# Merging the first two rounds of a staged attention and expert kernel, with two weight products made once

## The chip, the cores and the metric

The kernel runs on one core of a Trainium2 chip (trn2). The metric is the device time of one execution in microseconds, as the median of several runs. The engines are TensorE (PE, with its weight loads shown as PEld), VectorE (DVE), ScalarE (ACT), GpSimd (POOL) and SyncE (SP), which here only issues DMAs. Each runs its own list of instructions in order; they wait for one another through semaphores.

## The reference

The input x is 8 batches of 512 tokens of width 128. Two blocks follow one another, each with a normalisation ahead and one behind, and a residual sum:

```
x = x + layernorm(attn(layernorm(x)))        # block A: one head of 128, rotary, causal
x = x + layernorm(ffn(layernorm(x)))         # block B
attn: q, k = rope(x wq), rope(x wk);  r = softmax(mask(q k^T / 128)) (x wv) wo
ffn:  h = rmsnorm(x, g1);  c = h w_down (128 -> 64)
      q, k, v = c wq, c wk, c wv   (16 heads of 4 channels, rotary on q and k)
      x = x + softmax(mask(q k^T / 2)) v w_up
      t = rmsnorm(x, g2);  the two best of 8 experts by softmax(t router_w), weights normalised
      y = x + sum over the two of gate * (silu(t w1) * (t w3)) w2      (128 -> 256 -> 128)
```

All products are in float32 except the 16-head scores, which use bfloat16 rows in which each float32 value is cut into three parts.

## The kernel before

The work on a batch is cut into four stages, named by a letter: **a** is block A's attention up to the normalised result; **p** is block B's normalisation, the 64-wide projections, rotary, the cut into bfloat16 parts, the turned queries and keys, and the row maxima of the first group of four heads; **m** is the 16-head attention's scores (maxima m_x, exponentials m_e, in four groups g of six jobs each, m_xgn and m_egs) and the first half of the value products; **f** is the rest of those products, w_up, the router, and the sending of token rows to DRAM sorted by expert. A tile phase then runs the experts over tiles of 128 rows and finishes the batches.

The stages are software pipelined over rounds. Round i does stage a of batch i, p of batch i-1, m of batch i-2 and f of batch i-3, as far as they exist. The rounds are "a", "ap", "apm", "apmf" (five times, four of them in a loop of two by two), "pmf" (m of batch 6), "mf" (m of batch 7, called the drain round below) and "f" (with tiles between). Eleven rounds in all.

In each round every engine works through a hand-written list of steps (ORDER for full rounds; FILL_ORDER, SECOND_ORDER, LEAD_ORDER, TRAIL_ORDER, DRAIN_ORDER, LAST_ORDER for "a", "ap", "apm", "pmf", "mf", "f"). A step named in several lists is one job: TensorE makes it into a PSUM bank, and ScalarE or VectorE empties it. There are two small banks (for all steps but scores), given out in turn in TensorE's order, and three wide ones for scores. A matmul step waits until its bank was emptied by the job two before it (small) or three before it (wide). "warmN" is N matmuls of ones that nobody reads. "x&y" means that two score jobs are issued interleaved.

The steps that the change and the prediction name:

- a_xT turns the normalised x; a_qkv0 to 3 make q, k, v (TensorE L957, emptied by ScalarE L1145); a_rope is on VectorE for batches 0 and 1 (L706 to L712), else on POOL; a_qT, a_kT turn them; a_s0 to 3 are the scores (L971), their maxima on VectorE (L1508) and exponentials on ScalarE (L1162); a_p0 to 2 turn the probabilities (L979); a_oT multiplies them with v (L986), ScalarE empties it into a_xT, and a_r multiplies that with wo (L993); VectorE divides by the sums (L1520), and a_rstat and p_rnorm normalise (with a power on POOL, L1302, between).
- p_x1 (POOL L1321), p_stats, p_norm, p_hT (turned, L921, scaled by g1 on emptying), p_cT (times w_down, L1004, 64 rows of result), p_qkv0 and 1 (L1010), p_keep, p_rope and p_cut (L675 to L695; for batch 0 the keys' half on POOL and the queries' half on VectorE, for the others both on POOL), p_slots (POOL L1335: six copies of key parts into k_rows), p_slot0 to 2 (ScalarE L1199: query parts into q_rows), p_k0, p_k1, p_q0, p_q1 (turned rows, L1024), p_x0 to 5 (maxima, L1421).
- m_cutg writes the maxima of group g into q_rows (VectorE L1564), m_shiftg turns those rows (L1036, copied by VectorE L1569), and the exponentials of group g (ScalarE L1216) follow it. f_up's sum is L1581, the router's logits arrive at L1589.
- plan0 to plan2 in the drain round (VectorE L1703 to L1725) compute the table of the first 25 tiles. SyncE (L749 to L762) waits for the last exponential score of the pmf round, loads w1 and w3 (L750, L751) and w2 (L753, eight transfers), then waits for plan1 (soon_placed), writes the table to DRAM (L758), waits, and reads it back into one partition (L762). TensorE's plan_soon waits for that and for the weights, and then reads 25 expert numbers into registers:

```
sp.wait_ge(soon_placed, 1)
... tile_table <- soon_u; wait soon_out; early_u <- tile_table ...
def read_soon():                      # TensorE's step plan_soon
    pe.wait_ge(soon_in, 16 * 2)
    pe.wait_ge(weights_in, 16 * N_WEIGHTS)
    experts.update(read_tiles(pe, 1, 0, EARLY, NE - 1))
```

## Time and profile before

| | us |
|---|---|
| Median of 3 runs | 697.23 (695.5 to 699.96) |
| The profiled execution, its own time | 696.38 |
| Its span in the profile | 694.2 |
| PE busy | 609.9 (88%) |
| DVE busy | 506.8 (73%) |
| ACT busy | 412.0 (59%) |
| POOL busy | 339.6 (49%) |

The span runs from the first to the last instruction; 2.2 us of the execution lie around it. Busy time of PE is modelled from pipelined matmuls, so a busy PE is not PE at its peak, and it counts the warm-up matmuls. "PEclk" is the granted clock of TensorE as a share of full speed (1.00 is 2.4 GHz, 0.50 is 1.2 GHz). A row of the timeline gives start, duration, engine, line, operation, what it writes and reads, its shape and how often it stands in a row; in brackets is the idle time of the engine before it, and what ended it. A float32 product shows as two instructions.

### The profile page before, as it was taken

The page shows a single profiled execution, that of the slowest core. Times are in us where ns is not written, and L with a number is a line of the kernel's source. Part 1 is how long each engine was busy: PE and PEld are TensorE (multiplying, and loading weights), DVE is VectorE, ACT ScalarE, POOL GpSimd, SP SyncE. Part 2 cuts the span into 40 slices and gives each one's busy share as a digit, 9 for nine tenths or more (in the row PEclk, how much of TensorE's full clock was granted, in tenths as well). Part 3 has the DMA queues.
Part 4 walks back from the last instruction along what each step waited for, and adds up shares of the span by engine and source line. Part 5 has one row for each costly group of instructions (what it writes and reads, how often), then busy time and mean ns, then how long its engine had stood idle before and what let it go on. Part 6 is the DMA issues. An engine that isn't in the chain of part 4 may idle for free.

```text
span 694.2 us, 15645 instructions
## 1 busy us (share of the span) xinstructions
PE 609.9 (88%) x5186; PEld 364.6 (53%) x5186; DVE 506.8 (73%) x1616; ACT 412.0 (59%) x826; POOL 339.6 (49%) x388
## 2 busy tenths in 40 slices
PE   8887599999999899999999999879998887899980
PEld 3444345455545455454544545434343486899970
DVE  4456877786897898689779878677688356457894
ACT  3223158566658656565765657454564676688971
POOL 0043246058527835752873565165014056767783
PEclk9988879999999999999999999977898999999995
DMA  6200000000100000010000001001232013345653
GB/s 174 78 0 1 0 1 1 2 1 1 35 2 1 14 23 1 1 35 3 1 19 19 1 1 35 2 2 36 77 109 70 14 58 111 99 113 166 176 156 91
DMA packets 35616, 30.05 MB, mean 43 GB/s; under 512 B 6160, under 2 KB 32720, under 8 KB 35520
## 3 DMA queue, kind: packets, MB, share of 16 engines
q1 hardware_dynamic: 31216, 19.65, 10.1%
q0 software_dynamic: 4320, 9.38, 4.0%
q8 instruction: 45, 0.74, 0.4%
q14 instruction: 35, 0.29, 0.1%
HBM read 17.54 MB, written 12.57 MB: 43 GB/s over the span
## 4 chain that ended last, share of the span: by engine, by line
PE 64%; DVE 14%; ACT 9%; issue 7%; POOL 5%; DVEq 0%; POOLq 0%; ACTq 0%
PE wide L1116 9%; PE small L933 7%; PE small L921 5%; PE wide L895 4%; PE wide L1125 4%; ACT pT L1216 4%; PE wide L868 4%; PE wide L886 4%; PE wide L843 3%; PE small L957 3%; PE wide L877 3%; PE small L986 3%; PE small L971 2%; DVE nmax L1421 2%; PE small L1010 2%
## 5 line engine op out<-in xcount | busy, mean ns | idle before, releaser
L1421 DVE TENSOR_REDUCE nmax<-wide 128x2 f32<-128x256 f32 (+3 forms) x256 | 200.1, 817 | 43.7 <-PE wide L886 42.5
L1216 ACT ACTIVATE pT<-wide 128x1024 f32<-128x1024 f32 (+1 forms) x192 | 161.6, 883 | 41.3 <-PE wide L895 40.4
L1360 POOL DMA_INDIRECT result_rows<-k_rows,dest x71 | 69.9, 984 | 49.5 <-DVE k_rows L1764 26.6
L933 PE MATMUL small<-pT,v_pad 128*5 128x512 f32 (+3 forms) x1024 | 85.2, 478 | 2.7 <-ACT pT L1216 2.7
L1351 POOL DMA_INDIRECT token_rows<-m_row,place_u x64 | 62.5, 977 | 45.4 <-issue 16.4
L1302 POOL TENSOR_TENSOR a_rstd<-a_ve,neg_half 128x4 f32<-128x4 f32 x16 | 16.5, 1029 | 117.3 <-DVE a_ve L1407 117.3
L895 PE MATMUL wide<-qT,kT 32*128 32x384 bf16 (+3 forms) x512 | 71.5, 312 | 0.0
L886 PE MATMUL wide<-kT,qT 32*128 32x256 bf16 (+3 forms) x512 | 70.5, 314 | 0.0
L877 PE MATMUL wide<-future_T,idb 128*128 128x128 bf16 (+1 forms) x384 | 62.6, 246 | 7.9 <-DVE nmax L1421 4.6
L868 PE MATMUL wide<-future_sb,idb 128*128 128x128 bf16 (+1 forms) x384 | 64.1, 250 | 5.7 <-ACT pT L1216 2.8
L1145 ACT ACTIVATE oT_g<-small 128x512 f32<-128x512 f32 x32 | 19.1, 597 | 79.7 <-PE small L933 79.7
L933 PEld LDWEIGHTS small<-pT,v_pad 128*5 128x5 f32 x1024 | 25.8, 92 | 59.8 <-issue 50.3
L1759 DVE TENSOR_TENSOR a_work<-a_work,wide 128x256 f32<-128x256 f32 x71 | 29.7, 418 | 32.6 <-PE wide L1125 16.7
L877 PEld LDWEIGHTS wide<-future_T,idb 128*128 128x128 bf16 x384 | 28.6, 99 | 36.4 <-issue 15.8
L1125 PE MATMUL wide<-a_p_sb,a_work 128*128 x284 | 43.2, 275 | 0.6 <-DVE k_rows L1764 0.6
L1116 PE MATMUL wide<-a_work,p_hT_sb 128*128 128x128 f32 x280 | 38.0, 279 | 4.8 <-ACT a_work L1242 3.5
L868 PEld LDWEIGHTS wide<-future_sb,idb 128*128 128x128 bf16 x384 | 29.8, 101 | 22.7 <-issue 11.5
L1116 PE MATMUL wide<-a_work 128*128 128x128 f32 x288 | 38.8, 278 | 2.4 <-issue 2.2
L1125 PEld LDWEIGHTS wide<-a_p_sb,a_work 128*128 128x128 f32 x284 | 37.3, 192 | 0.8 <-issue 0.8
L1116 PEld LDWEIGHTS wide<-a_work,p_hT_sb 128*128 128x128 f32 x280 | 34.0, 192 | 7.0 <-ACT a_work L1242 4.4
L1116 PEld LDWEIGHTS wide<-a_work 128*128 128x128 f32 x288 | 35.3, 193 | 3.4 <-issue 3.0
L895 PEld LDWEIGHTS wide<-qT,kT 32*128 32x128 bf16 x512 | 20.1, 92 | 29.6 <-issue 16.8
(254 smaller groups left out, 1260.6 us busy)
## 6 DMA issues: line engine op xcount, KB each, us to landing
a_qkv_sb<-token_rows SPq DMA_DIRECT2D x71, 72.0 KB, 1.8
x<-L_attn_x SPq DMA_DIRECT2D x8, 256.0 KB, 3.4
w<-L_ffn_w SPq DMA_DIRECT2D x2, 1024.0 KB, 7.3
out<-x SPq DMA_DIRECT2D x16, 128.0 KB
result_rows<-k_rows,dest POOLq DMA_INDIRECT x71, 2.6
token_rows<-m_row,place_u POOLq DMA_INDIRECT x64
a_p_sb<-L_ffn_w SPq DMA_DIRECT2D x8, 128.0 KB, 4.6
yin_own<-result_rows SPq DMA_DIRECT2D x8, 128.0 KB
```

The lines of the kernel that those rows point to most:

```text
L868: pe.matmul(bank[:, i * T + lo:i * T + lo + len(blocks) * P], idb[:, :], future_sb[:, 0:len(blocks), :], start=True, stop=False, skip_grou ...
L877: pe.matmul(diagonal, idb[:, :], future_T[:, :, :] if len(blocks) > 1 else future_T[:, 0, :], start=True, stop=False, skip_group_check=True)
L886: return pe.matmul(bank_of(ring, max_name(g, n))[:, at:at + keys], qT1[rows, m.parity, g, tile * P:(tile + 1) * P], kT[rows, m.parity, g, ...
L895: return pe.matmul(bank_of(ring, exp_name(g, s))[:, at:at + queries_from(tile)], kT[rows, m.parity, g, tile * P:(tile + 1) * P], qT2[rows, ...
L921: last = pe.transpose(bank[0:rows, t * P:(t + 1) * P], source(t), ident)
L933: last = pe.matmul(bank[32 * r:32 * r + HD + 1, k * P:T], v_pad[:, m.parity, k, g * R + r, :], probs, start=(k == 0), stop=(k == NT - 1), ...
L1116: last = pe.matmul(wide[:, tile.half, j * P:(j + 1) * P], w_now[tile.half][:, j * P:(j + 1) * P], x_T[:, tile.half, :], start=True, stop=True)
L1125: last = pe.matmul(y_bank(tile), hid_T[:, tile.half, h * P:(h + 1) * P], w2_sb[:, e, h, :], start=(h == 0), stop=(h == FH - 1))
L1216: act.activation(pT[:, g % 2, part, at:at + n].rearrange("p (n q) -> p n q", n=2), in_, ACT.Exp, scale=SCALE_B).then_inc(ring.free(step), 1)
L1351: pool.indirect_dma_start(token_rows[:, :], bass.IndirectOffsetOnAxis(ap=place_u[:, n, t:t + 1], axis=0), m_row[:, n, t, :], None).then_in ...
L1360: pool.indirect_dma_start(result_rows[:, :], bass.IndirectOffsetOnAxis(ap=dest[:, tile.buf:tile.buf + 1], axis=0), y_rows[:, tile.buf, :], ...
L1421: ins = dve.tensor_reduce(nmax[:, tile, heads], bank[:, :, at:at + keys_up_to(tile)], AX, ALU.max, negate=True)
```

## The change

Four things are changed together.

1. The rounds "a" and "ap" are one round, "bap": b is stage a of batch 0, a is stage a of batch 1, and p is stage p of batch 0. The "a" list's steps of batch 0 are named b_... and mapped by of_first. Ten rounds remain. In this round VectorE has the keys' half of p_rope and p_cut and also the six key copies (p_slots), POOL has the queries' half.
2. fold0 makes wv wo once (turn wv, copy, multiply, copy; TensorE and ScalarE take turns), so that v already holds v wo. a_oT is gone, and a_r is ten products of 128x128x128 with the probabilities as the stationary operand. fold1 makes w_down [wq wk wv] once into wqkv_f (128x192). p_cT is gone, and p_qkv multiplies p_hT with wqkv_f.
3. wo is loaded with the first group of weights, ahead of the cosine and sine tables; batch 1's x has a semaphore of its own (x_second).
4. The lists of all rounds but "f" are laid anew. In the drain round plan_soon moves from the end of TensorE's list to the place behind m_e01, and plan1 on VectorE from behind m_shift1 to behind m_cut0.

The diff, cut to its core (the POOL and ACT lists of the other rounds, and the ends of long ones, are left out):

```diff
 ORDER = {   "PE"
-        m_x1_0 m_shift0 f_pv2 f_o1 m_e00&m_x1_1 f_pv3 f_o2 m_e01&m_x1_2 m_x1_3 a_xT f_o3 m_x1_4 a_qkv0 m_x1_5
-        f_oT a_qkv1 a_qkv2 a_qkv3 m_e02&m_x2_0 f_up p_hT m_x2_1 m_shift1 m_e03 m_e04 p_cT m_e05&m_x2_2 p_qkv0
-        a_qT m_x2_3 f_tT m_e10&m_x2_4 m_e11 f_logits p_qkv1 a_kT m_e12&m_x2_5 m_pv0 a_s0 m_e13 a_s1 m_e14 m_e15
-        a_s2 a_s3 f_rank m_x3_0 m_x3_1 m_pv1 m_shift2 m_x3_2 a_p0 m_e20 m_e21 p_k0 m_e22&m_x3_3 p_k1 p_q0
+        m_x1_0 m_shift0 f_pv2 f_o1 m_e00&m_x1_1 f_pv3 m_e01&m_x1_2 f_o2 m_x1_3 a_xT f_o3 m_x1_4 a_qkv0 a_qkv1
+        a_qkv2 a_qkv3 m_e02&m_x1_5 f_oT m_e03 f_up m_x2_0 m_x2_1 m_shift1 p_hT m_x2_2 p_qkv0 m_e04&m_x2_3 m_e05
+        f_tT m_e10&m_x2_4 f_logits m_e11 p_qkv1 m_e12&m_x2_5 a_qT a_kT m_pv0 m_e13 a_s0 a_s1 a_s2 a_s3 m_e14
+        m_e15&m_x3_0 m_x3_1 f_rank m_pv1 m_shift2 a_p0 m_e20&m_x3_2 m_e21 p_k0 m_e22&m_x3_3 p_k1 p_q0
...
-FILL_ORDER = {   "PE"
-        warm18 warm11 a_xT a_qkv0 a_qkv1 a_qkv2 a_qkv3 warm5 a_qT warm3 warm2 a_kT a_s0 a_s1 warm1 a_s2 a_s3
-        warm7 a_p0 a_p1 warm1 a_p2 warm2 a_oT warm3 a_r warm35
-SECOND_ORDER = {   "PE"
-        warm1 warm2 warm4 warm4 p_hT p_cT p_qkv0 p_qkv1 a_xT a_qkv0 a_qkv1 a_qkv2 warm5 a_qkv3 p_k0 warm3 p_k1
-        warm2 p_q0 warm1 a_qT p_q1 a_kT warm3 a_s0 a_s1 p_x0 warm1 a_s2 a_s3 p_x1 p_x2 warm2 p_x3 a_p0 a_p1
-        warm1 a_p2 p_x4 a_oT p_x5 a_r
...
+FIRST_ORDER = {
+    "PE": """
+        warm18 fold0 b_xT b_qkv0 b_qkv1 b_qkv2 b_qkv3 warm11 warm5 b_qT b_kT warm3 b_s0 b_s1 warm2 b_s2 b_s3
+        a_xT b_p0 b_p1 warm1 b_p2 b_r warm3 warm2 warm1 warm2 a_qkv0 a_qkv1 warm5 warm5 fold1 warm5 a_qkv2
+        a_qkv3 p_hT warm1 p_qkv0 p_qkv1 warm5 warm2 a_qT a_kT a_s0 a_s1 warm5 a_s2 a_s3 warm5 warm3 a_p0 warm2
+        warm1 warm3 a_p1 p_k0 a_p2 p_k1 p_q0 p_q1 a_r p_x0 p_x1 warm1 p_x2 p_x3 p_x4 p_x5""",
+    "ACT": """
+        fold0 b_xT b_qkv0 b_qkv1 b_qkv2 b_qkv3 b_qT b_s0 b_s1 b_s2 b_s3 a_xT b_p0 b_p2 fold1 a_qkv0 a_qkv1
+        a_qkv2 a_qkv3 p_hT p_keep p_qkv0 p_qkv1 a_qT a_s0 a_s1 p_slot0 p_slot1 a_s2 a_s3 p_slot2 a_p0 a_p2 p_q0
+        p_q1""",
+    "DVE": """
+        b_stats b_norm a_stats a_norm b_rope b_kT b_s0 b_s1 b_s2 b_s3 b_p1 b_r b_rstat p_rnorm p_stats p_norm
+        p_ms a_rope a_kT a_s0 a_s1 p_rope a_s2 a_s3 p_cut p_slots a_p1 p_k0 p_k1 a_r p_x0 a_rstat p_x1 p_x2 p_x3
+        p_x4 p_x5""",
+    "POOL": """
+        b_rstd a_rstd b_rrstd p_x1 p_rstd p_rs p_rope p_cut p_slots a_rrstd""",
 LEAD_ORDER = {   "PE", then "DVE"
-        m_x1_0 m_x1_1 a_xT m_x1_2 a_qkv0 m_x1_3 m_x1_4 m_shift0 a_qkv1 m_x1_5 a_qkv2 a_qkv3 m_e00&m_x2_0 m_x2_1
+        m_x1_0 m_shift0 m_x1_1 m_x1_2 a_xT m_e00&m_x1_3 a_qkv0 p_hT m_e01 m_e02&m_x1_4 a_qkv1 a_qkv2 m_x1_5
...
-        m_cut0 m_x1_0 p_rnorm a_stats p_stats a_norm m_x1_1 m_x1_2 p_norm m_x1_3 p_ms m_shift0 a_rope m_x1_4
+        p_rnorm m_cut0 a_stats m_x1_0 m_shift0 p_stats a_norm m_x1_1 p_norm m_x1_2 m_x1_3 m_x1_4 p_ms m_x1_5
 TRAIL_ORDER = {   "PE", then "DVE"
-        m_x1_0 m_shift0 f_pv2 f_o1 m_e00&m_x1_1 f_pv3 f_o2 f_o3 m_e01&m_x1_2 f_oT m_x1_3 p_hT f_up m_x1_4 p_cT
-        m_e02&m_x1_5 p_qkv0 p_qkv1 m_x2_0 f_tT m_shift1 f_logits m_e03&m_x2_1 m_e04 m_e05 m_e10 m_e11
+        m_x1_0 f_pv2 m_shift0 f_o1 m_e00&m_x1_1 f_pv3 m_e01&m_x1_2 f_o2 m_e02 f_o3 m_x1_3 f_oT m_e03&m_x1_4 f_up
+        m_e04&m_x1_5 m_e05 p_hT p_qkv0 p_qkv1 f_tT f_logits m_x2_0 m_x2_1 m_pv0 f_rank m_x2_2 m_x2_3 m_x2_4
+        m_shift1 m_e10&m_x2_5 m_e11 p_k0 m_x3_0 m_e12&m_x3_1 p_k1 m_e13&m_x3_2 m_e14 m_shift2 m_x3_3
...
+        p_rnorm m_cut0 m_shift0 p_stats m_x1_0 f_o1 m_x1_1 p_norm f_o2 f_o3 m_x1_2 m_x1_3 m_x1_4 p_ms f_up
+        m_x1_5 f_ms m_cut1 f_logits f_route0 p_rope f_route1 m_x2_0 f_route2 f_route3 f_at f_rank m_x2_1 m_x2_2
 DRAIN_ORDER = {   "PE", then "DVE"
-        f_pv2 f_o1 m_x1_0 m_x1_1 f_pv3 m_shift0 m_x1_2 f_o2 f_o3 m_e00&m_x1_3 m_x1_4 f_oT m_e01&m_x1_5 f_up
-        m_x2_0 m_e02&m_x2_1 m_e03 m_shift1 m_x2_2 m_e04&m_x2_3 f_tT m_e05 m_e10 m_e11 m_e12 m_e13 f_logits m_e14
...
-        m_e22 m_e23 m_shift3 m_e24 m_e25 m_e30 m_e31 m_e32 m_e33 m_o0 m_e34 m_e35 plan_soon""",
+        f_pv2 m_x1_0 f_o1 m_shift0 m_x1_1 f_pv3 f_o2 m_e00&m_x1_2 m_e01 plan_soon f_o3 m_e02&m_x1_3 m_x1_4 f_oT
+        m_e03&m_x1_5 f_up m_e04 m_e05 m_shift1 m_x2_0 m_pv0 m_e10 f_tT m_e11 m_e12 f_logits m_e13 m_e14
+        m_e15&m_x2_1 m_x2_2 m_x2_3 f_rank m_pv1 m_x2_4 m_x2_5 m_x3_0 m_shift2 m_x3_1 m_o0 m_e20&m_x3_2 m_x3_3
...
-        plan0 m_cut0 m_x1_0 f_o1 m_x1_1 m_shift0 m_x1_2 f_o2 f_o3 m_x1_3 m_x1_4 m_x1_5 f_up m_cut1 m_x2_0 f_ms
-        m_x2_1 m_x2_2 m_x2_3 m_shift1 plan1 f_logits f_route0 f_route1 f_route2 f_route3 f_at m_x2_4 f_rank
+        plan0 m_cut0 plan1 f_o1 m_x1_0 m_x1_1 m_shift0 f_o2 m_x1_2 f_o3 m_x1_3 m_x1_4 m_x1_5 f_up m_cut1
+        m_shift1 f_ms m_x2_0 f_logits f_route0 f_route1 f_route2 f_route3 f_at f_rank f_count m_x2_1 m_x2_2
+def of_first(step, a, ring):
+    return ("a" + step[1:], Batch(0, 0), ring.of_first()) if step[0] == "b" else (step, a, ring)
-        FIRST = ("a", "ap", "apm", "apmf")
+        FIRST = ("bap", "apm", "apmf")
+        FOLDS = ((wqkv_a[:, 2 * D:3 * D], m_tT[:, 0:P], wo_sb[:, :], wqkv_a[:, 2 * D:3 * D], P, D),
+                 (wdown_sb[:, :], oT_sb[:, 0:P], wqkv_b[:, :], wqkv_f[:, :], L, 3 * L))
+        def key_slots(eng, p):
+            k = k_rows[:, :, :, :, :].rearrange("p t h s d -> p (t h) s d")
+            for b, slots in ((part1, (0, 3, 5)), (part2, (1, 4)), (part3, (2,))):
+                for s in slots:
+                    last = eng.tensor_copy(k[:, :, s, :], b[:, 1, :, :])
+            last.then_inc(S["p_rows"], 1)
+            def fold(n):                                        (TensorE)
+                left_, turned, right, _, rows, cols = FOLDS[n]
+                pe.wait_ge(*((first_in, 16 * N_FIRST), (consts_in, 16 * N_CONSTS))[n])
+                pe.transpose(wide[0:rows, 1 + n, 0:P], left_, idf[:, :]).then_inc(folded, 1)
+                pe.wait_ge(folded, 4 * n + 2)
+                pe.matmul(wide[:, 1 + n, T:T + cols], turned, right, start=True, stop=True).then_inc(folded, 1)
-                    elif step == "a_oT":
...
+                    elif step == "a_r":
                         bank = take(ring, step, ["a_p0", "a_p1", "a_p2"])
+                        for i in range(NT):
+                            for k in range(i + 1):
+                                n, at = ((0, 0), (1, 0), (2, 0), (1, 3 * P))[k]
+                                at += (i - k) * P
+                                last = pe.matmul(bank[:, i * P:(i + 1) * P], a_pT[:, n, at:at + P],
+                                                 a_qkv[:, k, 2 * D:3 * D], start=(k == 0), stop=(k == i),
+                                                 skip_group_check=True)
-                    elif step == "p_cT":
-                        bank = take(ring, step, ["p_hT"])
-                        full(ring, step, pe.matmul(bank[0:L, :], wdown_sb[:, :], p_hT[:, :], start=True, stop=True))
-                            last = pe.matmul(bank[:, at:at + 3 * L], p_cT[:, t * P:(t + 1) * P], wqkv_b[:, :],
+                            last = pe.matmul(bank[:, at:at + 3 * L], p_hT[:, t * P:(t + 1) * P], wqkv_f[:, :],
+            def fold(n):                                        (ScalarE)
+                _, turned, _, product, rows, cols = FOLDS[n]
+                act.wait_ge(folded, 4 * n + 1)
+                act.activation(turned, wide[0:rows, 1 + n, 0:P], ACT.Copy).then_inc(folded, 1)
+                act.wait_ge(folded, 4 * n + 3)
+                act.activation(product, wide[:, 1 + n, T:T + cols], ACT.Copy).then_inc(folded, 1)
```

## Rows read from the trace of the kernel before

**Rows 1.** Busy time by stretch: span, busy us (instructions), PEclk, DMA, GB/s.
```profile
0.00:36.00 36.00, 30.34 (x129) 14.80 (x130) 15.81 (x55) 10.40 (x19) 2.32 (x7) 1.00 0.41 121
36.00:80.83 44.83, 36.28 (x188) 20.18 (x186) 29.67 (x82) 14.67 (x33) 13.32 (x20) 0.89 0.00 1
80.83:136.66 55.83, 48.32 (x408) 24.97 (x408) 41.58 (x103) 34.21 (x59) 23.96 (x30) 0.88 0.01 1
...
197.02:255.85 58.83, 55.24 (x518) 30.12 (x518) 49.48 (x138) 38.27 (x73) 34.55 (x40) 1.00 0.04 11
...
436.57:497.50 60.93, 52.78 (x459) 24.22 (x458) 42.49 (x101) 31.69 (x56) 25.78 (x31) 0.80 0.04 11
497.50:543.60 46.10, 41.03 (x388) 17.66 (x386) 35.55 (x116) 24.67 (x40) 10.87 (x11) 0.89 0.31 96
...
```

**Rows 2.** TensorE timeline; last, instructions of L1145 (ns min/median/max, starts).
```profile
246.74 2.42 PE L986 MATMUL small<-a_work,a_qkv_sb 128*128 128x512 f32 x8
...
252.39 1.16 PE L993 MATMUL small<-wo_sb,a_xT_sb 128*128 128x128 f32 x8
...
215.28 1.07 PE L1004 MATMUL small<-p_hT_sb,wdown_sb 128*64 128x512 f32 x2
...
L1145 ACT ACTIVATE p_cT_sb<-small x8: 573/591/592, 45.2 to 453.5; 64x512 f32<-64x512 f32 x8
```

**Rows 3.** Timeline of the first two rounds.
```profile
14.67 0.69 DVE L706 TENSOR_TENSOR a_work<-a_qkv_sb,cos_a_sb 128x512 f32<-128x512 f32 x1 [5.63 <-ACT a_qkv_sb L1145]
...
32.48 0.69 DVE L1520 TENSOR_TENSOR a_xn<-small,a_ri 128x512 f32<-128x512 f32 x1 [4.79 <-PE small L993]
...
45.98 2.10 PE L1010 MATMUL small<-wqkv_b_sb,p_cT_sb 64*128 64x192 f32 x8 [0.77 <-ACT p_cT_sb L1145]
...
55.83 3.42 POOL L1335 COPY k_rows<-part 128x256 bf16<-128x256 bf16 x6
```

**Rows 4.** Timeline of VectorE: two casts of 128x256, without and beside POOL's work.
```profile
8.75 0.28 DVE L1434 CAST future_T<-pT 128x256 bf16<-128x256 f32 x1
...
53.27 0.57 DVE L691 CAST part<-p_t 128x256 bf16<-128x256 f32 x1
```

**Rows 5.** Busy time by stretch within the third round.
```profile
80.83:86.00 5.17, 0.00 (x0) 0.00 (x0) 4.93 (x25) 0.00 (x0) 3.30 (x3) 0.51 0.00 0
86.00:98.00 12.00, 10.56 (x50) 5.10 (x51) 9.04 (x24) 3.98 (x7) 2.86 (x3) 0.64 0.01 2
```

**Rows 6.** Timeline of ScalarE: the first exponential of all.
```profile
97.10 1.02 ACT L1216 ACTIVATE pT<-wide 128x1024 f32<-128x1024 f32 x1
```

**Rows 7.** Busy time by stretch within the pmf round.
```profile
459.00:478.00 19.00, 16.79 (x117) 6.90 (x118) 13.57 (x36) 7.98 (x11) 15.28 (x21) 0.55 0.04 13
```

**Rows 8.** Timeline of VectorE in the drain round: f_up's sum, and the logits.
```profile
510.94 0.69 DVE L1581 TENSOR_TENSOR res<-small,res 128x512 f32<-128x512 f32 x1
...
520.31 0.19 DVE L1589 COPY lgs<-small 128x32 f32<-128x32 f32 x1 [0.44 <-PE small L1059]
```

**Rows 9.** Timeline of SyncE in the drain round; then its waits (us, times, longest).
```profile
498.81 8.05 SPq L753 DMA_DIRECT2D a_p_sb<-L_ffn_w  x8
...
525.39 0.51 SPq L762 DMA_DIRECT2D a_qkv_sb<-tile_table  x2
...
SPq L762 <- DMA tile_table<-a_xT_sb: 4.8, 1, 4.8
...
SPq L639 <- DMA a_qkv_sb<-tile_table: 2.1, 1, 2.1
```

**Rows 10.** Timeline of VectorE in the drain round: m_cut0, and plan1's first and last.
```profile
500.85 0.23 DVE L1564 TENSOR_TENSOR q_rows<-nmax 128x16 bf16<-128x16 f32 x1
...
516.62 0.18 DVE L1667 TENSOR_TENSOR a_kT_sb<-a_kT_sb 128x32 f32<-128x32 f32 x1
...
519.72 0.14 DVE L1696 TENSOR_SCALAR a_xT_sb<-a_xT_sb 128x1 uint32<-128x1 f32 x1
```

**Rows 11.** Timeline of TensorE in the tile phase, where it reads 24 registers.
```profile
589.64 1.13 PE L1116 MATMUL wide<-a_work 128*128 128x128 f32 x8 [1.87 <-issue]
```

200 lines of the change are left out of this document (100 added, 100 removed).

## The prediction

> **What bounds the kernel now.** I first cut the span into rounds at the first cut of the maxima (m_cut0, L1564) of each batch and read the busy time by stage [rows 1]. The stages have different limits. In a full round (all four stages; there are five, and the one shown is typical of 58.8 to 60.8 us) TensorE is busy 55.24 of 58.83 us at a granted clock of 1.00, with VectorE at 49.48 and ScalarE at 38.27: there a microsecond less of TensorE work is nearly a microsecond of time. The first two rounds are another thing: 36.00 us and 44.83 us in which VectorE works 15.81 and 29.67 us; one batch's chain of dependent steps sets them, and 117 warm-up matmuls fill much of TensorE's row. The third round (80.83 to 136.66) and the pmf round (436.57 to 497.50) show a clock of 0.88 and 0.80, so they lose time to gaps and to the clock after them. In the drain round (mf) VectorE is busy 35.55 of 46.10 us, and the last exponentials follow its maxima. The tile phase, all that lies behind 543.6, is not touched: its list is the same and its inputs come in the same form.
>
> **Less TensorE work in each round.** a_oT and a_r (eight and eight instructions, 2.42 and 1.16 us [rows 2]) become one a_r of ten 128x128x128 products, or twenty instructions. The row of 1.16 us has eight of this shape, 0.145 each: 20 x 0.145 = 2.9 us against 3.58, so -0.7. The step p_cT (1.07 us) goes whole; p_qkv keeps its eight instructions of 192 columns, only with 128 rows contracted in place of 64. No row shows that form; the nearest with 128 rows is the one of 0.145 for 128 columns, so 0.22 for 192 and 1.7 for eight, against the 2.10 that the eight take at 45.98 at a lower clock [rows 3]: no loss is in sight, and I take no change. That is -1.8 us in a round with a and p. ScalarE loses the evacuations of a_oT and p_cT (0.59 us each [rows 2]) and their two hand-overs; it isn't the bound, so I count these at nothing in a full round. VectorE keeps its work, which was 49.5 of 58.8 us, so it does not become the bound at 57 us. Five full rounds: 5 x -1.8 = -9. From below and above: -3.5 if new gaps (the four a_s jobs now stand back to back on TensorE with two small banks between them) eat 1.1 us a round, and -12 if the hand-overs count too.
>
> **The merged first round.** The old chain of batch 0: a_r reaches VectorE at 32.48, p_qkv runs at 45.98, the keys' slots are copied on POOL from 55.83 for 3.42 us, and the stage ends with m_cut0 at 80.83 [rows 1, 3]. In the new list fold0 (a transposition, a copy, a product, a copy, some 1.5 us) stands after 18 warm-ups in place of 29, so batch 0's transposes start about 0.6 us earlier, if wo, now the fifth transfer of the first group, has landed; its issue moves ahead of the two tables. Dropping a_oT takes its evacuation and hand-overs, 1.1 us, besides the 0.7. With a_xT of batch 1 ahead of b_p0 on ScalarE costing back 0.6, a_r arrives at about 30.8 (-1.6). Without p_cT (1.07 + 0.59 + two hand-overs of 0.2) p_qkv moves by 3.5 in all. But then VectorE has batch 1's work in the way: a_rope (14.67 to 18.75 for batch 0, so 4.1 us), a_kT, a_s0 and a_s1 stand ahead of p_rope, and p_cut and the six key copies follow it on VectorE. Adding these up from 41.3: rope to 45.4, a_kT to 48.2, a_s1 to 50.4, p_rope to 52.9, a_s2 and a_s3 to 54.4, p_cut to 57.5. The six copies on VectorE aren't in the trace: a cast of 128x256 there took 0.28 us with POOL idle and 0.57 beside POOL's work [rows 4], so 1.7 to 3.4 us; POOL has finished its half by then, so I take 2 and have them at 59.5, where the old kernel had 59.25. After that p_k, p_q, a_r and a_rstat and the six p_x maxima (6.3 us) follow in a row, with nothing of the next round between: p_x5 at about 75.5. So the merge brings -5.3, not the 10 that the overlap of two 36 to 45 us rounds suggests, because VectorE's list is serial. Bounds: -3 (copies at 0.57, p_x waiting on a_r's 2.9 us of matmuls) to -9 (VectorE waits less than I put).
>
> **Third round.** In the first 5.17 us TensorE did nothing, then it ran 12.00 us at a clock of 0.64 [rows 5]: its list held m_shift0 back behind a_qkv0, so the first exponential came at 97.10, 16.3 us into the round [rows 6]. Now m_shift0 is second, p_rnorm is done early, and m_e00 stands right after a_xT, which needs VectorE's a_stats, p_stats and a_norm, some 7 us. Filling the gap and the clock's loss (12.00 x 0.36 = 4.3) is worth up to 9.5 with the 1.8 of work; a_xT still waits, so I take half, -5 (0 to -9).
>
> **The pmf round.** It has no a stage and yet lasts 60.93 us, longer than a full round. From 459 to 478 the clock was 0.55 [rows 7]: 16.79 us busy, some 7 more than at full clock. p_cT's 1.07 goes; m_e02 to m_e05 come earlier, so that TensorE has denser work up to the p stage, but f_logits on VectorE now follows m_cut1 with only m_x1_5 and f_ms before it, and must wait for the row-norm chain (9.4 us from f_up's sum to the logits in the drain round [rows 8]). Gains and this wait partly cancel: -5 (+2 to -11).
>
> **The drain round, the part that goes the wrong way.** plan_soon was TensorE's last step; now it stands after m_e01. It waits for the tile table to have been through DRAM. The table can't be early: SyncE issues the eight w2 transfers until 506.86, and only then looks at the table. From its two writes, some 0.65 us of issue, it waited 4.8 us for them, took 0.51 to issue the second trip and 2.1 until it landed [rows 9]: 506.9 + 8.1 = 515.0, or 17.5 us after the round's start at 497.5. TensorE gets there sooner: plan0 ends with m_cut0 at 500.85, plan1 takes 516.62 to 519.86, so 3.2 us [rows 10], moved ahead of f_o1: VectorE is through with it at 504.3. One o-normalisation (0.5), two maxima of about 1.2 and a copy of 0.4 make 507.8, and TensorE's f_o2, m_e00 with m_x1_2, and m_e01 (estimates from the same timeline: the small ones 0.6 each, the pair 1.4) make 510.4. So TensorE stands still for 4.6 us and then reads 25 registers; the gap in the tile phase where 24 are read was 1.87 us [rows 11]. Queued behind it on TensorE are f_o3, m_e02, m_x1_3 and all maxima, and so VectorE and ScalarE, which run dry after m_x1_2 and m_e01. That is +6.5. Before, this reading lay beside the last exponentials and cost nothing. Also the wait for the logits loses its cover, since m_x2_1 to m_x2_5 now follow f_count: I add 2 (up to 5), less 0.5 for the register reads that leave the end. Drain: +8 (+3 to +12).
>
> The Trainium skill ("DMA: Bandwidth & Descriptors", Anatomy of one DMA) says that a DMA has about 2.0 us of fixed cost, most of it the receipt of the write. By that page the two trips would take about 4 us behind their issues and not 6.9, and the drain would cost about 5 in place of 8. For the trip back this trace agrees (2.1 us); for the one into DRAM it doesn't (4.8 us), and the measurement decides.
>
> **The sum** goes against the profiled execution, 696.38 us with a span of 694.2: -5.3 - 5 - 9 - 5 + 8 = -16.3, a span of 677.9, and 2.2 around it give 680.1. The median of the runs, 697.23, is 0.85 above the profiled one, so 681.
>
> **Rivals.** *The drain's wait is hidden* (0.17): TensorE arrives at plan_soon later than I put, or what it delays isn't needed. For it: TensorE idled 5 of 46 us there before. Then 681 - 8 = 673. *Only the removed work counts* (0.20): the new lists bring nothing in the third and pmf rounds beyond 1.8 and 1.1 us. Against it stands the clock of 0.51 and 0.64; for it, that a chain through VectorE (41.6 of 55.8 us busy) binds anyway. -5.3 - 1.8 - 9 - 1.1 + 8 = -9.2, or 688. *Slower, by the clock in the full rounds* (0.07): there TensorE idled 3.6 us of 58.8 in short pieces at a clock of 1.00. The relaid lists put p_hT directly before p_qkv0 and a_s0 to a_s3 together, and with less work the pieces grow; after longer gaps (80.83 to 86) the trace shows a stretch at 0.64, and after those around 457 one at 0.55. 55.24 us of work at a mean clock of 0.88 as in the third round costs 7.5 us more, five times 37; it needs 16.3 + 7 = 23.3, or 4.7 us in each of five rounds (a clock near 0.92), to come out slower by 1%. Then 704 and more. The Trainium skill ("TensorE: Matmul & The Clock Gate", Part 1) has the clock throttled by default and released by activity, which is what this rival would need and what the two slow stretches agree with.
>
> **Chances and range.** Forecast 0.56, hidden wait 0.17, only the work 0.20, slower 0.07. The forecast's own bounds (full rounds -3.5 to -12, merge -3 to -9, third 0 to -9, pmf +2 to -11, drain +3 to +12) added as independent errors give about 10 either way, 671 to 691. With the other cases I say 668 to 694. Faster by over 1% (about what a measurement of this kernel can tell from no change), under 690.3: 0.80; within 1%: 0.13; slower: 0.07.
>
> **What would show it.** Right: full rounds of about 57.5 us; no instruction of p_cT or a_oT and twenty of 0.145 in a_r; m_cut0 of batch 0 near 75.5; its first exponential within 10 us of that; TensorE idle for 4 to 7 us some 13 us into the drain round, ended by the DMA of the tile table. Wrong: full rounds still at 59 or more (the list made new gaps), a drain round of 46 us, or a granted clock under 0.95 in the full rounds.

## The result, and the profile after

The changed kernel is slower: 712.16 us (median of 4 runs, 707.98 to 714.79) against 697.27 for the kernel before (4 runs beside it); ratio 1.0205, 95% interval 1.0142 to 1.0267. The forecast was 681. Its profiled execution took 710.8 us with a span of 708.9, 14.7 more than the 694.2 of before.

First the busy time by stretch of the changed kernel, cut as in [rows 1]: at the m_cut0 of each batch, then the drain round and the tile phase. The columns are stretch and length, then busy us (instructions) of PE, PEld, DVE, ACT and POOL, then clock, DMA share and GB/s.

```profile
0.00:36.00 36.00, 30.41 (x137) 15.78 (x138) 19.96 (x75) 11.55 (x24) 4.59 (x9) 1.00 0.42 121
36.00:69.68 33.68, 24.82 (x162) 14.54 (x160) 24.91 (x72) 12.48 (x30) 8.49 (x12) 0.92 0.00 1
69.68:128.92 59.24, 51.28 (x414) 28.19 (x414) 39.72 (x99) 33.55 (x57) 22.89 (x29) 0.85 0.01 1
...
189.20:249.40 60.20, 54.81 (x520) 29.74 (x520) 51.99 (x137) 37.21 (x70) 33.83 (x40) 0.97 0.04 11
249.40:311.13 61.73, 55.41 (x520) 30.72 (x520) 51.83 (x138) 37.87 (x71) 34.98 (x41) 0.94 0.03 11
311.13:369.81 58.68, 53.12 (x520) 29.32 (x520) 51.79 (x138) 37.21 (x70) 34.38 (x40) 1.00 0.04 11
...
430.96:497.40 66.44, 51.81 (x454) 24.57 (x454) 39.44 (x97) 31.51 (x54) 24.77 (x30) 0.78 0.03 10
497.40:558.20 60.80, 48.78 (x390) 20.72 (x386) 37.30 (x122) 24.25 (x39) 10.86 (x11) 0.75 0.25 73
```

- The first m_cut0 is at 69.68 where it was at 80.83: -11.2 (forecast -5.3).
- Third round: 59.24 for 55.83, +3.4 (forecast -5).
- The five full rounds together: 302.0 for 299.9, +2.1 (forecast -9). TensorE's busy time did fall, 55.2 to 56.8 us a round before and 52.8 to 55.4 now; but its idle time rose from 3.7 to 6.6 us a round, and VectorE's busy time from about 49.2 to 51.8.
- pmf round: 66.44 for 60.93, +5.5 (forecast -5). Drain round: 60.80 for 46.10, +14.7 (forecast +8).
- Tile phase: 150.70 for 150.60.

The experiments are read from m_cut0 to m_cut0: by that cut pmf is +5.3 and all from the drain's m_cut0 to the end +15.0 (208.4 for 193.4), and the five terms make 14.7. One thing shifts this cut: in the new list of the pmf round p_rnorm stands ahead of m_cut0 on VectorE. The last full round takes 61.15 us with that list behind it (61.14 to 61.16 in e1, e2 and e8) and 58.98 with the old one (e5; 58.97 in e12), so some 2.2 us of the "five full" belong to the pmf round where its new list is run.

Next, the drain round of the changed kernel around plan_soon: SyncE's issues and TensorE.

```profile
504.53 3.94 PE L954 MATMUL small<-pT,v_pad 128*5 128x512 f32 x32 [2.82 <-DVE o_tok L1621]
505.97 0.72 SPq L779 DMA_DIRECT2D tile_table<-a_xT_sb  x2
509.91 0.39 PE L916 MATMUL wide<-qT,kT 32*128 32x512 bf16 x2
512.03 0.51 SPq L783 DMA_DIRECT2D a_qkv_sb<-tile_table  x2
516.62 1.57 SPq L793 DMA_DIRECT2D a_qkv_sb<-token_rows  x3
516.67 1.09 PE L942 MATMUL small<-idf,oT_g 128*128 128x128 f32 x4 [6.37 <-issue]
```

TensorE reached plan_soon at 510.3, stood still for 6.37 us and resumed at 516.67: the forecast had 510.4, and 4.6 plus 1.87 us. From the table's two writes SyncE waited 5.3 us before the trip back (4.8 in [rows 9]), then 1.9. The new item is the first line: plan1 stands ahead of f_o1 on VectorE, so f_pv3 waited 2.82 us for the o-normalisation and then ran at a granted clock of 0.59 (504.5 to 508.5), 3.94 us for 32 instructions that take 2.34 at full clock.

VectorE in the merged round:

```profile
29.34 0.69 DVE L1565 TENSOR_TENSOR a_xn<-small,a_ri 128x512 f32<-128x512 f32 x1 [2.90 <-PE small L1022]
...
39.56 0.69 DVE L727 TENSOR_TENSOR a_work<-a_qkv_sb,cos_a_sb 128x512 f32<-128x512 f32 x1
...
53.16 0.91 DVE L715 COPY k_rows<-part 128x256 bf16<-128x256 bf16 x6
...
61.23 1.21 DVE L1455 TENSOR_REDUCE nmax<-wide 128x2 f32<-128x1024 f32 x1
```

The first a_r arrived at 29.34 (put at 30.8), batch 1's a_rope began at 39.56 (41.3), the six key copies on VectorE took 0.91 us in all (2) and ended at 54.1 (59.5). From there to m_cut0 it was 15.6 us (16.0). The last line is the first maximum of stage p (p_x0), which begins that tail.

### The profile page after: what moved, and what is told of

Read it like the earlier page. It is cut to its first block, busy times and chain, and to the rows that moved or that the text cites. A ratio compares the mean times of both kernels' runs of the same rounds, so it can differ in the third digit from the quotient of the medians.

```text
span 708.9 us, 15634 instructions
## 1 busy us (share of the span) xinstructions
PE 596.0 (84%) x5182; PEld 362.4 (51%) x5182; DVE 515.1 (73%) x1622; ACT 406.2 (57%) x814; POOL 336.1 (47%) x381
## 4 chain that ended last, share of the span: by engine, by line
PE 47%; DVE 25%; issue 11%; ACT 6%; POOL 6%; SPq 2%; DMA 2%; DVEq 0%; POOLq 0%; ACTq 0%
DVE nmax L1455 7%; PE wide L1145 7%; PE small L954 5%; PE wide L916 4%; PE small L942 4%; PE wide L898 4%; PE wide L1154 3%; PE small L1022 3%; PE wide L889 3%; PE small L992 3%; ACT pT L1252 2%; PE small L1006 2%; PE wide L907 2%; PE small L1053 2%; DVE a_xn L1445 2%
## 5 line engine op out<-in xcount | busy, mean ns | idle before, releaser
L1252 ACT ACTIVATE pT<-wide 128x1024 f32<-128x1024 f32 (+1 forms) x192 | 163.5, 882 | 85.7 <-PE wide L916 84.2
L1394 POOL DMA_INDIRECT result_rows<-k_rows,dest x71 | 69.9, 984 | 54.2 <-DVE k_rows L1809 30.8
L907 PE MATMUL wide<-kT,qT 32*128 32x256 bf16 (+3 forms) x512 | 72.4, 321 | 0.0
L898 PE MATMUL wide<-future_T,idb 128*128 128x128 bf16 (+1 forms) x384 | 64.7, 253 | 8.0 <-DVE qT L1614 4.1
L1174 ACT ACTIVATE oT_g<-small 128x512 f32<-128x512 f32 x32 | 19.1, 597 | 64.9 <-PE small L954 64.8
L1804 DVE TENSOR_TENSOR a_work<-a_work,wide 128x256 f32<-128x256 f32 x71 | 29.7, 418 | 35.2 <-ACT a_work L1284 19.1
L1145 PE MATMUL wide<-a_work,p_hT_sb 128*128 128x128 f32 x280 | 38.0, 279 | 3.7 <-ACT a_work L1278 1.8
L1145 PE MATMUL wide<-a_work 128*128 128x128 f32 x288 | 38.7, 277 | 2.3 <-issue 2.1
L1145 PEld LDWEIGHTS wide<-a_work,p_hT_sb 128*128 128x128 f32 x280 | 34.0, 192 | 6.0 <-issue 3.7
L1145 PEld LDWEIGHTS wide<-a_work 128*128 128x128 f32 x288 | 35.1, 192 | 3.3 <-issue 2.9
```

The source lines that it names most:

```text
L898: pe.matmul(diagonal, idb[:, :], future_T[:, :, :] if len(blocks) > 1 else future_T[:, 0, :], start=True, stop=False, skip_group_check=True)
L907: return pe.matmul(bank_of(ring, max_name(g, n))[:, at:at + keys], qT1[rows, m.parity, g, tile * P:(tile + 1) * P], kT[rows, m.parity, g, ...
L1145: last = pe.matmul(wide[:, tile.half, j * P:(j + 1) * P], w_now[tile.half][:, j * P:(j + 1) * P], x_T[:, tile.half, :], start=True, stop=True)
L1252: act.activation(pT[:, g % 2, part, at:at + n].rearrange("p (n q) -> p n q", n=2), in_, ACT.Exp, scale=SCALE_B).then_inc(ring.free(step), 1)
L1394: pool.indirect_dma_start(result_rows[:, :], bass.IndirectOffsetOnAxis(ap=dest[:, tile.buf:tile.buf + 1], axis=0), y_rows[:, tile.buf, :], ...
L1804: dve.tensor_tensor(hid_T[:, tile.half, :], silu[:, tile.half, :], wide[:, tile.half, F:2 * F], ALU.mult)\
```

## The experiments

Two things are told apart in all of them: the steps (a_oT and p_cT gone, the merged round) and the four relaid lists. "Old" is the list of the kernel before without p_cT and a_oT. The stages of every profiled execution, from m_cut0 to m_cut0, in us; the last column runs from the drain's m_cut0 to the end of the span. The ratios of e9 to e12 stand against fewer runs of the kernel before, so their intervals are wider:

| run | median | ratio (95%) | third | five full | pmf | to the end |
|---|---|---|---|---|---|---|
| before | 697.3 | | 55.8 | 299.9 | 64.3 | 193.4 |
| changed | 712.2 | 1.021 (1.014 to 1.027) | 59.2 | 302.0 | 69.6 | 208.4 |
| e1 old drain | 690.3 | 0.988 (0.981 to 0.995) | 56.2 | 304.5 | 70.3 | 192.4 |
| e2 plan_soon last | 702.2 | 1.005 (1.001 to 1.009) | 56.2 | 303.6 | 69.2 | 200.0 |
| e3 four old lists | 704.4 | 1.011 (1.006 to 1.016) | 59.4 | 321.5 | 59.6 | 191.9 |
| e4 old full list | 725.6 | 1.041 (1.033 to 1.048) | 59.2 | 320.0 | 65.4 | 208.0 |
| e5 old pmf, drain | 686.5 | 0.981 (0.976 to 0.986) | 56.1 | 302.8 | 64.6 | 194.0 |
| e6 e4 + 14 dummies | 710.4 | 1.017 (1.011 to 1.024) | 57.7 | 311.3 | 64.0 | 206.8 |
| e7 e5 + TensorE dummies | 689.4 | 0.988 (0.984 to 0.992) | 57.7 | 309.1 | 59.4 | 198.5 |
| e8 e2 + plan1 back | 698.4 | 0.999 (0.996 to 1.003) | 57.7 | 303.6 | 70.3 | 196.9 |
| e9 new list, old steps | 718.3 | 1.033 (1.020 to 1.045) | 56.9 | 316.2 | 69.6 | 192.4 |
| e10 e4 + 6 dummies | 709.5 | 1.019 (1.006 to 1.031) | 57.7 | 305.6 | 64.4 | 211.5 |
| e11 e5 + VectorE dummy | 710.9 | 1.023 (1.010 to 1.037) | 56.0 | 323.2 | 65.1 | 194.5 |
| e12 e5 + 7 in third | 680.9 | 0.978 (0.966 to 0.990) | 56.7 | 304.3 | 59.6 | 194.1 |

A stage whose code and whose predecessors are the same in several kernels (the third round of the changed kernel, e1, e2, e4 to e8, e10, e11) still lies between 56.0 and 59.2, so a difference of 3 us in one stage of one profile says nothing by itself. These ten lie in three groups by the granted clock of the stage: 59.2 us at 0.85 (two), 57.7 at 0.87 (four) and 56.0 to 56.2 at 0.90 (four). The first full round does the same: 60.3 us at 1.00 (changed), 61.7 at 0.97 (e8), 64.3 at 0.92 (e1, e2, e5, e12). So stages are best compared at equal clock.

**The drain round.** First its whole list undone, for all four engines:

```
 DRAIN_ORDER: the four engines' lists of the kernel before
```

> The changed kernel with one edit undone: the lists of the drain round (mf), of all four engines, are those of the kernel before. The two lists name the same steps, so nothing else moves. My theory: the 14.7 us that the drain round became longer (46.10 to 60.80) are all the list's: the round is back at 46 to 47.5 us and the kernel at 712.2 - 14.7 = 697.5 (695 to 700). Rival: the longer drain comes from what the rounds ahead leave behind (a later SyncE, which starts the table's transfers only after the w2 transfers, or a TensorE clock that is already low): then the drain stays over 54 us and the kernel at 706 or more.

Measured: 690.3 us, from m_cut0 to the end 192.4 for 208.4. All of the longer drain is the list's; the rounds ahead leave nothing behind that lengthens it. The kernel is 7 us faster than before with that one list back. To the end, the old drain list took 191.9 to 198.5 us in eight profiles and the new one as it stands 206.8 to 211.5 in four.

```
 DRAIN_ORDER["PE"]
-    ... m_e00&m_x1_2 m_e01 plan_soon f_o3 m_e02&m_x1_3 ...
+    ... m_e00&m_x1_2 m_e01 f_o3 m_e02&m_x1_3 ... m_e34 m_e35 plan_soon
```

> The changed kernel, with plan_soon alone put back at the end of TensorE's list of the drain round; plan1 on VectorE and all else of the new drain list stay. Theory A (the term of the prediction): the stall of TensorE at plan_soon, 6.37 us idle and some 1.9 us in which the registers are read, is most of the 14.7: 8 to 10 us come back, a drain of 51 to 53 us, the kernel at 702 to 704. Theory B: the wait only shifts slack, and the new order of VectorE (plan1 ahead of f_o1, the routing in one piece without cover) sets the end: 0 to 4 us come back, a drain of 57 to 61 us, the kernel at 708 to 712. If more than 12 us come back, the stall took the clock down with it and is the whole cause.

Measured: 702.2 us, 200.0 to the end, so plan_soon is 8.4 of the 16.0 us by which the changed kernel lies behind e1. That is theory A, near its lower size: the stall of 6.37 us and a clock that it takes down (this run's drain had 0.81 where the changed one had 0.75):

```profile
495.10:548.00 52.90, 45.52 (x390) 19.56 (x386) 37.23 (x122) 25.13 (x40) 10.84 (x11) 0.81 0.29 84
```

Then plan1 as well:

```
 DRAIN_ORDER["DVE"], on top of e2
-    plan0 m_cut0 plan1 f_o1 ... m_shift1 f_ms m_x2_0 f_logits
+    plan0 m_cut0 f_o1 ... m_shift1 f_ms m_x2_0 plan1 f_logits
```

> The run with plan_soon last (702.2 us, drain 52.9 us), and in it plan1 moved back on VectorE, to just ahead of f_logits. It splits the 6.8 us that this drain is longer than the old one. Theory A (plan1's 3.2 us ahead of f_o1 delay the whole f chain): 4 to 6 us come back, 696 to 698. Theory B (the routing steps in one piece, with m_x2_1 to m_x2_5 behind them, leave VectorE waiting for the logits): 0 to 2 us come back, 700 to 702.

Measured: 698.4 us, 3.8 less (ten runs each), and 3.1 less in the profile, which alone would be within its spread: just under theory A's 4 to 6, above B's 2. VectorE's logits show both halves, in e2 and in e8:

```profile
520.13 0.19 DVE L1634 COPY lgs<-small 128x32 f32<-128x32 f32 x1 [3.94 <-PE small L1088]
```
```profile
520.70 0.18 DVE L1634 COPY lgs<-small 128x32 f32<-128x32 f32 x1
```

In e2 they are read 21.9 us after m_cut0 and VectorE has waited 3.94 us for them; in e8 19.1 us after it, and the wait is filled by plan1. What is left between e8 and e1, which differ in the drain list alone, is 4.5 us in the profiles (196.9 and 192.4) and 8.1 in the medians. It belongs to what else the list moves (m_x2_1 to m_x2_5 behind f_count, the exponentials ahead of the maxima); which of it was not tried.

**The full rounds.** The changed kernel with the old list in the five full rounds, and with all four old lists:

```
 ORDER: the four engines' lists of the kernel before, less p_cT and a_oT
```

> The changed kernel with only the list of the five full rounds as before (less p_cT and a_oT). Theory A (the relaid list of the full rounds eats the saving): five rounds take 291 in place of 302 us, the kernel 701 (699 to 704). Theory B (the saving is hidden, the list is neutral): five rounds take 300 to 302 us and the kernel 710 to 712. VectorE's busy time in a full round tells where: 49.5 us as before or 51.9 as in the changed kernel, if its longer instructions come from where POOL's steps now lie.

> The changed kernel's merged first round, its weight products and its copies of the keys, but with the lists of the full rounds, the third round, the pmf round and the drain round as they were before, only without p_cT and a_oT (a_r stands where it stood). Theory A: the removed work is worth what I put, 1.8 us in each round with a and p stages and 1.1 in the pmf round, and the relaid lists ate it: 697.2 - 11.2 (first rounds, as measured) - 6 x 1.8 - 1.1 = 674 (671 to 678). Theory B: the removed work was hidden behind the chain through VectorE; the old lists give just the old rounds back: 697.2 - 11.2 = 686 (684 to 689). The full rounds tell them apart: 58.1 us each (290.5 for five, from 299.9 less 9) or 60.

Measured: 725.6 and 704.4 us, and neither theory: the full rounds came out at 64.0 and 64.3 us each, longer than the 60.0 of the kernel that does more work in the same order. Laid on the round from 197.02 of [rows 1], each counted from its m_cut0, e4's round from 194.11 loses its time in two places. Its first 6 us have a clock of 0.50 (f_pv2 takes 4.45 us for 2.34), and from there it runs some 2.5 us late, steadily, up to 52 us into the round. Then comes the place where a_oT stood ([rows 2], 246.74), behind which it loses 4.9 more. TensorE of e4 (and VectorE's reading of a_r) there, and the stretches around it:

```profile
247.84 0.28 PE L898 MATMUL wide<-future_T,idb 128*128 128x128 bf16 x2 [1.54 <-DVE qT L1614]
...
253.30 4.64 PE L1022 MATMUL small<-a_qkv_sb,a_work 128*128 128x128 f32 x20
...
257.98 0.69 DVE L1565 TENSOR_TENSOR a_xn<-small,a_ri 128x512 f32<-128x512 f32 x1 [4.41 <-PE small L1022]
```
```profile
243.00:249.00 6.00, 4.23 (x41) 2.28 (x40) 5.82 (x11) 2.76 (x6) 3.61 (x4) 0.95 0.19 64
249.00:258.00 9.00, 9.00 (x48) 6.41 (x46) 3.40 (x9) 2.74 (x3) 0.00 (x0) 0.50 0.00 0
```

TensorE waits 1.54 us for VectorE's copy of m_shift3, and then runs 9 us at a clock of 0.50, the lower level of 1.2 GHz. The new a_r takes 4.64 us there (2.50 at full clock), VectorE stands 4.41 us for it, and the next round starts late. Before, a_oT's 2.42 us lay in that wait. The wait, 1.54 to 1.63 us, stands in all five full rounds of e4, and the clock over 14 us at the end of each is 0.63, 0.63, 0.76, 0.88 and 0.76; in the kernel before there is no such wait and the five clocks are 1.00. If this is the cause, work that computes nothing must help:

```
 ORDER["PE"], on top of e4
-    m_e03 m_e04 m_e05&m_x2_2 ... p_x2 m_e30&p_x3
+    m_e03 m_e04 warm4 m_e05&m_x2_2 ... p_x2 warm10 m_e30&p_x3       (e6)
+    m_e03 m_e04 m_e05&m_x2_2 ... p_x2 warm6 m_e30&p_x3              (e10)
```

> The run with the old list of the full rounds (725.6 us, full rounds of 60.7 to 66.1 us, clock 0.87 to 0.97) with dummy products where the removed steps stood on TensorE: 4 of 512 columns for p_cT and 10 for a_oT. They compute nothing that is used and hand nothing over. Theory clock: the removed products had kept TensorE's clock up while VectorE was behind; with dummies in their place the full rounds are back at 59.5 to 61 us at a clock of 0.97 or more, the kernel at 700 to 708, though TensorE does 2 to 3 us more in each round. Theory order (the old list waits somewhere on the new steps, whatever the clock): the dummies add their own time, rounds of 64 us or more and the kernel at 725 or above.

> The changed kernel with the old list of the full rounds (725.6 us without dummies, 710.4 with 4 and 10), now with 6 dummy products of 512 columns alone, where a_oT stood. Theory clock: the gap in which TensorE waits for the copy of m_shift3, behind the place of a_oT, is what lets the clock fall, so 6 are enough: full rounds of 59.5 to 61.5 us, 703 to 709, less than with 14 dummies. If each dummy helped by itself (some effect along the whole round), 6 of 14 would give 716 to 720.

Measured: 710.4 and 709.5 us; full rounds 62.3 and 61.1 us in place of 64.0. So dummies make the kernel 15 to 16 us faster, and six in the one gap do as much as fourteen (e6 misses the 700 to 708 of the clock theory, e10 its 703 to 709 by 0.5; in e6 the dummies themselves may be in the way, TensorE being busy 58.5 of 62.3 us). The same place in e10:

```profile
361.56 1.47 PE L864 MATMUL wide<-ones 128*128 128x512 bf16 x6
363.03 0.28 PE L898 MATMUL wide<-future_T,idb 128*128 128x128 bf16 x2
...
366.53 2.50 PE L1022 MATMUL small<-a_qkv_sb,a_work 128*128 128x128 f32 x20
```

No wait ahead of the future_T product, and a_r at 2.50. It is so in all five rounds of e10, and the clock at their ends is 1.00 five times. The second round of e4 and of e10, the last 14 us:

```profile
246.00:260.00 14.00, 12.13 (x72) 7.54 (x72) 8.13 (x21) 4.21 (x5) 1.22 (x2) 0.63 0.04 12
```
```profile
238.00:252.00 14.00, 13.35 (x122) 7.67 (x118) 11.87 (x31) 8.01 (x11) 3.41 (x4) 1.00 0.07 23
```

The Trainium skill ("TensorE: Matmul & The Clock Gate", Part 1) says that the throttled state is the default and that activity releases it; these rows agree.

The fourth cell beside old list with old steps, old with new and new with new:

```
 kernel before, ORDER relaid as in the change, with
+    PE:  ... p_hT m_x2_2 p_cT m_e04&m_x2_3 p_qkv0 ... p_x1 a_p2 m_e30 a_oT m_o0 ...
+    ACT: ... p_hT p_cT m_e04 p_qkv0 ... a_p2 m_e25 m_e30 a_oT m_e31 ...
```

> The kernel before with one edit: the list of the full rounds is the relaid one, with p_cT put in behind m_x2_2 and a_oT behind m_e30 (on ScalarE behind p_hT and behind m_e30). It is the fourth cell beside old list and old steps (60.0 us a full round), old list and new steps (64.0) and new list and new steps (60.4 and 60.6). Theory A (the removed TensorE work is worth its 1.8 us a round where the list fits it): 62 to 63 us a full round, the kernel 707 to 714. Theory B (VectorE's list sets the full round, TensorE's work lies beside it): 59.5 to 61 us a full round, the kernel 695 to 702.

Measured: 718.3 us, 63.2 us a full round, theory A and beyond. The five full rounds by steps and list:

| | old list | new list |
|---|---|---|
| old steps | 299.9 | 316.2 |
| new steps | 320.0 to 321.5 | 302.0 to 304.5 |

In the relaid list the removed steps are worth 12 to 14 us, more than the 9 forecast (they take two copies of ScalarE and their hand-overs with them, so it isn't TensorE's time alone); in the old one they cost 20. And the relaid list costs the old steps 16. So neither the steps nor the list has a worth of its own; only the pair has. Where I put a_oT and p_cT was my choice, so the 316.2 is that of one placing.

**Which engine sets a full round.** Dummy work of about equal size on either engine, at the same place of e5's list:

```
 ORDER, on top of e5
+    PE:  ... p_x1 a_p2 warm10 m_e30 ...                             (e7)
+    DVE: ... m_x3_5 a_p1 idle m_cut3 ...                            (e11)
+    idle: dve.tensor_reduce(spare, cos_a_sb broadcast to 4 x 512, AX, ALU.max)
```

> The run with the old pmf and drain lists, and 10 dummy products of 512 columns (some 2.2 us of TensorE at full clock) in each full round, ahead of m_e30, where the kernel before had a_oT. Theory A (TensorE does not bound the full rounds of the new list; VectorE's list does, so the removed work brought nothing): the five rounds change by less than 1 us each, the kernel within 4 us of the run without the dummies. Theory B (TensorE bounds, as the prediction had it): 5 x 2.2 = 11 us slower.

> The run with the old pmf and drain lists (686.5 us), and in each full round one dummy maximum over 2048 columns on VectorE ahead of m_cut3, some 2.2 us, whose result is not used. It is the counterpart of the 10 dummy products on TensorE, which cost 2.9 us in all. Theory A (VectorE's list sets the full round): nearly all of it shows, 1.5 to 2.2 us a round, 7 to 11 us in all, 694 to 698. Theory B (TensorE sets it, or the two share it): 0 to 1 us a round, under 691.

Measured: 689.4 us with the ten products (+2.9 in the median, +6.3 in the profile's full rounds, for 12 us of added work by six taking 1.47), and 710.9 with VectorE's dummy: +24 us for 5 x 2.28 = 11.4, far over theory A's 694 to 698. Behind that dummy TensorE waits 1.82 us and falls to half clock, as in e4:

```profile
302.79 2.28 DVE L1600 TENSOR_REDUCE spare<-cos_a_sb 128x4 f32<-128x2048 f32 x1
...
305.32 0.44 PE L1065 MATMUL small<-idb,q_rows 128*128 128x128 bf16 x4 [1.82 <-DVE q_rows L1612]
```
```profile
306.00:312.00 6.00, 5.64 (x31) 2.48 (x30) 3.64 (x5) 2.81 (x4) 0.00 (x0) 0.50 0.03 12
```

So the two runs differ in the clock too, and the totals don't say which engine sets a round. Rounds of the same list at the same place and clock do it better. Third full round at 1.00: e7 61.2 us, e1, e2, e8 and e12 59.4 to 59.7. Fourth at 1.00: e7 60.6, the changed kernel, e2 and e5 58.7. First at 0.92: e11 65.5, e1, e2, e5 and e12 64.3. At equal clock, then, TensorE's 2.4 us show with 1.5 to 1.9 and VectorE's 2.28 with 1.2. So neither engine alone sets the round. If the other rounds are like the first, VectorE's own share of e11's 24 us is about 6, and the rest is the clock, 0.92 in each of its five rounds. Each dummy was tried at one place only.

ScalarE wasn't tried at all, though more of TensorE's idle time ends with it than with VectorE. The longest waits of TensorE in the five full rounds of the changed kernel (us in total, times, longest):

```profile
PE small L1065 <- DVE q_rows L1610: 6.3, 10, 1.5
PE wide L889 <- ACT pT L1252: 4.5, 14, 0.6
PE small L1039 <- ACT p_hT_sb L1174: 3.7, 5, 0.8
PE wide L898 <- DVE qT L1614: 3.0, 8, 0.7
PE small L1006 <- ACT a_p_sb L1202: 2.8, 5, 0.6
```

Of all that are listed, ScalarE ends 17.3 us and VectorE 11.6; before, 9.2 and 6.6. L1039 is p_qkv0 waiting for p_hT's copy and L1006 an a_s job waiting for its bank: both are the list's doing, since e9 has them too (3.7 and 2.7, the first with p_cT in the place of p_qkv0) and the kernel before has neither.

**The pmf round.** Old pmf and old drain list, all else as changed:

> The changed kernel with the lists of the pmf round and of the drain round as they were before (less p_cT); merged first round, weight products, and the new lists of the third and the full rounds stay. The theory that the four lists are separate terms: the run with the old drain list alone was at 690.3 with a pmf round of 66.95 us, and the run with all old lists had a pmf round of 56.31 us, so 690.3 - 10.6 = 680 (676 to 684), pmf 56 to 58 us. Rival (the short pmf round needs the old full round ahead of it, or a slower clock eats it): pmf stays above 62 us and the kernel at 686 to 691. At 680 it is faster than both kernels.

Measured: 686.5 us, 3.8 less than e1 and short of the 10.6 that I had added up, as the rival had it; pmf 64.6 for 70.3 in this profile, but 59.4, 65.1 and 59.6 in e7, e11 and e12, which have the same list there. What splits these is a pause of TensorE as the round begins, in which it waited for nothing that the profile shows:

```profile
431.54 0.42 PE L1064 MATMUL small<-idb,q_rows 128*128 128x128 bf16 x4 [3.51 <-issue]
```
```profile
431.07 0.40 PE L1064 MATMUL small<-idb,q_rows 128*128 128x128 bf16 x4 [0.51 <-DVE q_rows L1609]
```

It is 3.51 us in e5 (the first line; the second is the same place in e12) and 3.08 in e11, and isn't there in e7, e12 and e3; what causes it is open. It comes with either list: 2.44 us before, 3.1 to 3.4 in the changed kernel, e1, e2 and e8, 2.1 in e4, none in e6 and e10. With the new steps and the pause the new pmf list gave 69.2 to 70.3 (65.4 in e4, behind the old full list) and the old one 64.6 and 65.1; without it the new one 64.0 and 64.4 (e6 and e10, behind the old full list) and the old one 59.4 to 59.6. So the new list costs some 5 us by this cut, and the pause about as much. What stands ahead moves this round too: with the old steps and the same old pmf list it took 64.3 us before and 69.6 in e9, at a clock of 0.68, where only the full rounds' list is changed.

**The third round.**

```
 LEAD_ORDER["PE"], on top of e5
-    m_x1_0 m_shift0 m_x1_1 m_x1_2 a_xT m_e00&m_x1_3 ...
+    m_x1_0 m_shift0 m_x1_1 m_x1_2 warm7 a_xT m_e00&m_x1_3 ...
```

> The run with the old pmf and drain lists (686.5 us), and 7 dummy products of 512 columns in the third round ahead of a_xT, where TensorE stood idle for 3.57 us and ran at a clock of 0.50 until 80. Theory clock: they lift the clock before the batch norms arrive; the stretch from 80 to 92 starts at full clock, m_e00 to a_qkv3 come 2 to 3 us earlier and the third round lasts 53 to 55 us, where the six profiles of this list so far showed 56.1 to 59.2. Rival (VectorE, 9.4 us busy in the first 10.3, sets the start whatever the clock is): the round stays at 56 to 59 us and the kernel within 2 us of 686.5.

Measured: the third round 56.7 us, so the rival stands for the round, though not for the kernel, which is 5.6 us faster and not within 2. The dummies did fill the head, 9.50 us busy where it was 6.41 (e12 first, then the changed kernel), and the clock rose a little earlier:

```profile
69.72:80.00 10.28, 9.50 (x45) 4.39 (x45) 9.39 (x34) 2.70 (x5) 3.33 (x3) 0.61 0.01 2
```
```profile
69.68:80.00 10.32, 6.41 (x30) 3.67 (x31) 9.38 (x34) 2.14 (x3) 3.32 (x3) 0.50 0.01 2
```

The kernel's 680.9 us is the lowest median of all, 2.2% below before, but its interval (0.966 to 0.990) holds e5's 0.981, and the third round isn't where it differs: of the two profiles e12's is 5.0 us shorter in the pmf round, where it lacks e5's pause of 3.51 us. That the seven dummies brought the faster kernel is not shown. e5 and e12 both beat both kernels.

## Why the prediction was wrong

**The full rounds' term, 5 x -1.8 = -9, failed: it takes removed TensorE time one for one and puts the relaid lists at nothing.** In the five rounds TensorE's busy time fell by 12.4 us (281.5 to 269.1), but its idle time rose by 14.5 (18.4 to 33.0), and that makes the +2.1; some 2.2 of it are the cut's, so the term came to about nothing in place of -9. I read from 55.24 us busy of 58.83 [rows 1] that a microsecond of TensorE's work is nearly a microsecond of time. Part of that busy share was filler in waits, as a_oT was ahead of m_shift3: in the old list the removal opened a wait and a clock of 0.50 and cost 20 us, in the relaid one it gave 12 to 14, and the relaid list by itself cost 16. The saving in TensorE's work was real (a_r 2.50 us for twenty instructions where I put 2.9, p_qkv 1.81 for 1.80). The new waits had been named: p_hT directly before p_qkv0 and a_s0 to a_s3 together are 6.5 of the idle time, 1.3 us a round, where my lower bound had 1.1 for new gaps and the forecast took none. The rival that had the clock in the full rounds got 0.07 and was placed in the wrong list: it is true of the removed work in the old list, while in the relaid one the clock is 0.94 to 1.00 in the changed kernel's rounds and 0.92 to 1.00 in e1, e2, e5, e8 and e12. That VectorE does not become the bound was neither right nor plainly wrong: at equal clock its dummy shows with about half.

**"VectorE keeps its work" was wrong by 2.6 us a round.** Some of its small steps, of the routing and into q_rows, now run beside POOL's rotations. VectorE and POOL in a full round of the changed kernel:

```profile
325.99 1.43 POOL L730 TENSOR_TENSOR a_work<-a_qkv_sb,sin_a_sb 128x256 f32<-128x256 f32 x2
325.99 0.81 DVE L1609 TENSOR_TENSOR q_rows<-nmax 128x16 bf16<-128x16 f32 x1
...
337.25 1.28 POOL L688 TENSOR_TENSOR p_t<-p_qk,cos_b_sb 128x512 f32<-128x512 f32 x1 [1.20 <-ACT v_pad L1225]
337.26 1.32 DVE L1502 TENSOR_TENSOR e_tmp<-lg,top 128x32 f32<-128x32 f32 x1
```

The two took 0.23 and 0.19 us in the round of before. The 1.32 us are about those of POOL's instruction, and the 0.81 lie beside two of POOL's that take 1.43 together. The Trainium skill ("SBUF — State Buffer", SBUF: two separate sides) says that the port pair which VectorE and GpSimd share is an exclusive lock for the whole instruction; the rows agree. The rise needs the new steps and the new list together: VectorE's busy time is 49.8 us a round in e4 and 49.7 in e9. It doesn't show as time, though: in the fourth full round VectorE is busy 51.79 us in the changed kernel and 50.53 in e2 and e5, and all three last 58.7; in e8 it is busy 49.46 there and the round lasts 61.3, at a clock of 0.94.

**The merged round: mechanism right, size too small.** -11.2 for -5.3, outside the bounds. The tail of the chain was right to 0.4 us; the chain up to the key copies was 5.4 us too long: the start of a_rope 1.7; the copies 1.1 (I took them from a cast of float32 values, 0.28 us; these read bfloat16 and took 0.15 each); and 2.6 between, of which p_cut is 1.0 (2.1 us, not 3.1) and the step to a_kT's copy 0.8 (2.0, not 2.8). The 41.3 us from which I added up and the 0.2 for a hand-over stand in no row, and the trace puts a_rope's start at 39.56.

**Third round: the head as forecast, the end not, and part of the +3.4 is the clock.** The first exponential came 8.7 us into the round (78.39; 16.3 before, "within 10" forecast). But "half of the gap and of the clock's loss is gained" fails: VectorE's first maximum of the attention scores, which heads the chain to a_r, came 30.0 us into the round before (110.83) and 29.9 after:

```profile
99.55 0.29 DVE L1553 TENSOR_REDUCE a_nm<-small 128x1 f32<-128x128 f32 x1 [0.84 <-PE small L1008]
```

The exponential came 7.6 us earlier and this chain only 0.1. With e12's fuller TensorE it came 28.7 us into the round, 1.1 earlier than in e5, and the round was no shorter (56.7 for 56.1). The changed kernel's 59.2 is of the slowest group of its list (0.85); at 0.90 the same list takes 56.0 to 56.2, level with the 55.8 of before at 0.88. The old list was run with the new steps only once there (e3: 59.4 at a clock of 0.83), so whether the new list gains anything in this round is not shown; the -5 isn't there in any profile.

**The pmf round: the wait I named was mis-sized, and the round's length misread.** I had put +2 to -11 and taken -5. The 60.93 us of before held a pause of TensorE of 2.44 us (at 438.48) that ends with nothing the profile shows; I had put the round's length down to the clock and the gaps alone, and the changed kernel's has 3.36. Waits of the changed kernel in this round (us in total, times, longest):

```profile
DVE nmax L1455 <- PE wide L907: 9.6, 8, 5.2
DVE lgs L1634 <- PE small L1088: 7.6, 1, 7.6
...
DVE qT L1614 <- PE small L1065: 6.0, 2, 5.5
```

VectorE waits 7.6 us for the logits, with f_route0 ahead of all maxima of m_x2; TensorE's clock was 0.78. That the wait is what makes the new list's 5 us is argued from the order of the steps; no run moved f_route0 alone.

**The drain round: right in its main term.** The stall was forecast to 0.1 us (6.5 for 6.37), TensorE's going on at 516.9 for 516.67, and without it 8.4 us came back. To hit it that closely was partly luck: the writes took 0.5 us more than put, and SyncE was at them 0.9 us sooner. The rival of a hidden wait falls. What was missed is the rest: I moved plan1 "ahead of f_o1" and used it only for when the table is ready, not for the f chain behind it (3.1), and put 2 us for the lost cover, where all else in the list cost 4.5 by the profiles.

The rival in which only the removed work counts shares the failed term. The sum failed less in any one term than in the sign of three: -9, -5 and -5 became +2.1, +3.4 and +5.3, and the one good surprise, 5.9 us in the merged round, covers the drain's miss of 7.0 almost.

## What to carry to other kernels

A high busy share doesn't make an engine the bound: ask what stands in its waits. Work removed from such a wait can let the clock fall and cost more than it saved. A known amount of dummy work on each engine shows what it costs, but only between rounds at the same granted clock: here the totals (+24 and +3 us) pointed at VectorE alone, and at equal clock both showed in part. A new order belongs to the steps that it was laid for, so steps and lists are to be timed in all four pairings, stage by stage: here the relaid full list earned its place only with the new steps, the third's was not settled, and those of the pmf and the drain round were losses with the new steps wherever both lists were run.

## What the runs showed of the hardware

- TensorE fell to a clock of 0.50 for 6 to 9 us behind waits as short as 1.54 and 1.82 us; with six products in the gap it was 1.00 there in five rounds of five (e10), against 0.63 to 0.88 without them (e4). I had looked for that only behind idle stretches like the 5.17 us of [rows 5].
- A VectorE instruction of 0.19 us took up to 1.32 us when it started beside a POOL instruction of 1.28.
- At the start of the pmf round TensorE paused for 2.1 to 3.5 us in eight of fourteen profiles, and waited there for nothing that the profile shows. With the same lists the round was some 5 us longer with the pause (64.6 and 65.1) than without (59.4 and 59.6).
- Two writes into DRAM, issued behind eight larger loads, cost 5.3 us until the next step could start, the trip back 1.9.
